# A GRU with the batch turned onto the partitions: split state, 256-column products, biases copied into PSUM, output in rows

## The reference, cut to what matters

```python
# x: [128, 32, 256] f32, cond: [128, 256]; b = 128 sequences of T = 32 steps, D = 256, 16 heads of 16
def block(x, emb):                                   # layer 0, for each sequence by itself
    scale, shift = split(emb @ W_emb + b_emb, 2)
    xn = rms_norm(x, g_norm) * (1.0 + scale) + shift
    q, k, v = heads(xn @ W_qkv)                      # q and k are rms-normed by head
    o = softmax(q @ k.T * 16 ** -0.5) @ v
    return o + o @ W_out
def gru(h, xs):                                      # layer 1, h starts as cond
    for x in xs:                                     # 32 steps
        gi, gh = x @ W_ih + b_ih, h @ W_hh + b_hh    # 256 -> 768 each: r, z, n
        r, z = sigmoid(gi.r + gh.r), sigmoid(gi.z + gh.z)
        n = tanh(gi.n + r * gh.n)
        h = (1 - z) * n + z * h
        yield h
x = x + block(x, cond);  return x + gru(cond, x)
```

## Time and profile before

| what | us |
|---|---|
| median of 3 runs (357.6 to 361.39) | 360.73 |
| the profiled execution's own time | 360.27 |
| span of the profiled execution | 358.5 |
| TensorE busy in the span (94%) | 337.3 |
| DVE, ACT, POOL busy | 251.7, 228.9, 205.2 |
| attention stage, until the last result transpose | 193 |
| first sigmoid of the recurrence | 196.9 |

### The profile page before, as it was taken

The page is one execution under the profiler, slowest core; times in us unless marked ns, Lnnn a source line. Parts: engine busy times, 40 slices in busy tenths (PEclk is TensorE's granted clock), DMA queues, the critical chain, the costliest instruction groups (busy, mean ns, idle before and its releaser), DMA issues.

```text
span 358.5 us, 12899 instructions
## 1 busy us (share of the span) xinstructions
PE 337.3 (94%) x4314; PEld 306.1 (85%) x4314; DVE 251.7 (70%) x637; ACT 228.9 (64%) x668; POOL 205.2 (57%) x381
## 2 busy tenths in 40 slices
PE   7797899999999999999689999999999999999990
PEld 6566788888888888888568999999999999999990
DVE  2658899899999999999775555555555555555554
ACT  3676778888888888876544555555655555655442
POOL 5477777787778777887412454434454444454331
PEclk9999999999999999999999999999999999999997
DMA  5963333232322233255310011211111111111112
GB/s 191 301 202 94 88 86 86 71 89 84 85 83 78 68 86 86 82 153 170 85 33 2 6 30 27 31 27 26 26 27 27 29 26 27 26 26 27 29 30 32
DMA packets 54768, 24.91 MB, mean 69 GB/s; under 512 B 40770, under 2 KB 49620, under 8 KB 54740
## 3 DMA queue, kind: packets, MB, share of 16 engines
q1 hardware_dynamic: 54036, 23.73, 26.7%
q10 hardware_dynamic: 704, 0.82, 0.6%
HBM read 7.48 MB, written 4.19 MB: 33 GB/s over the span
## 4 chain that ended last, share of the span: by engine, by line
PE 80%; SPq 7%; DMA 4%; DVE 2%; POOL 2%; issue 2%; ACT 1%; POOLq 0%; ACTq 0%
PE bank L1047 37%; PE bank L1099 24%; PE bank L1187 4%; PE bank L1206 4%; PE bank L1175 4%; SPq L394 4%; SPq L386 4%; DMA operands<-operands 2%; PE bank L1158 2%; PE bank L1167 2%; DMA w_emb_sb<-in_L_cond_W_emb_dram 1%; PE bank L1066 1%; PE bank L1112 1%; PE bank L1053 1%; POOL operands L457 1%
## 5 line engine op out<-in xcount | busy, mean ns | idle before, releaser
L1099 PE MATMUL bank<-h,w_hh_sb 128*128 128x128 f32 x768 | 95.6, 279 | 0.2
L1099 PEld LDWEIGHTS bank<-h,w_hh_sb 128*128 128x128 f32 x768 | 90.8, 191 | 2.5 <-DVE h L1034 0.8
L1019 DVE SCALAR_TENSOR_TENSOR operands<-bank,vec_cols,operands 128x128 f32<-128x128 f32 x64 | 22.2, 347 | 46.9 <-ACT operands L766 46.9
L1047 PE MATMUL bank<-pair_hi,wih_hi 128*128 128x256 f32 x180 | 52.6, 292 | 0.0
L766 ACT ACTIVATE operands<-bank,bsum 128x128 f32<-128x128 f32 x64 | 23.0, 359 | 46.1 <-PE bank L1099 45.1
L554 POOL TENSOR_TENSOR operands<-operands,h 128x128 f32<-128x128 f32 x64 | 29.6, 463 | 38.3 <-ACT operands L767 38.3
L1047 PE MATMUL bank<-pair_lo,wih_hi 128*128 128x256 f32 x180 | 50.2, 279 | 0.0
L1047 PE MATMUL bank<-pair_hi,wih_lo 128*128 128x256 f32 x180 | 50.1, 278 | 0.0
L563 POOL TENSOR_TENSOR operands<-h,x2T 128x256 f32<-128x256 f32 x31 | 22.5, 727 | 46.7 <-issue 34.1
L1047 PE MATMUL bank<-wqkv_hi,xn_hi 128*128 128x256 f32 (+1 forms) x126 | 47.3, 376 | 0.4 <-POOL xn_lo L486 0.3
L1047 PE MATMUL bank<-wqkv_lo,xn_hi 128*128 128x256 f32 (+1 forms) x126 | 42.4, 336 | 0.0
(11 more groups left out here) (125 smaller groups left out, 855.0 us busy)
## 6 DMA issues: line engine op xcount, KB each, us to landing
v_diag<-v_rows SPq DMA_DIRECT2D x128, 34.0 KB, 1.9
operands<-operands SPq DMA_DIRECT2D x64, 64.0 KB, 2.0
operands<-operands SPq DMA_DIRECT2D x32, 128.0 KB, 2.1
out_dram<-operands SPq DMA_DIRECT2D x254, 16.0 KB, 1.4
x_in<-in_x_dram SPq DMA_DIRECT2D x7, 512.0 KB, 8.9
stage_w<-in_L_cond_W_ih_dram SPq DMA_DIRECT2D x1, 768.0 KB, 5.6
w_hh_sb<-in_L_cond_W_hh_dram SPq DMA_DIRECT2D x1, 768.0 KB, 5.6
w_emb_sb<-in_L_cond_W_emb_dram ACTq DMA_DIRECT2D x1, 512.0 KB, 5.0
```

Of the source, the lines that this page charges most:

```text
L1019: dve.scalar_tensor_tensor(out=rh[:, c, :], in0=xnh[:, HN_COL:HN_COL + B], scalar=bhh[:, 2 * KC + c:2 * KC + c + 1], in1=r_g[:, c, :], op0 ...
L1047: last = pe.matmul(dst, a, w, start=start and i == 0, stop=i == len(terms) - 1, skip_group_check=True)
L1099: last = pe.matmul(dst, gate(w_hh_sb, name, c)[k], moving, start=k == 0 and (name == "n" or opens and name == "z"), stop=k == KC - 1, skip ...
```

## The change

h lies with the batch on partitions, four steps of it in turn. In each step TensorE transposes its two halves (`turned`), ACT writes the high part of each transposed half, DVE the low part, and these are the stationary operands; the weights of w_hh, split into parts in the place of w_qkv, move with 256 columns (r and z of a chunk side by side, or n). So 18 state products in fp32r replace 12 in fp32. The input products have the same turned form, one time step at a time; 13 of the 18 stand before the first transpose, 5 between the two. They belong to the step's own time, not to the next pair. The biases no longer enter as bias columns: products of a row of ones with the bias rows make them in PSUM once for each of two sets of banks, a copy is kept, and in each step ACT copies those of r and z into the banks of the next step, and DVE those of n. z serves for both uses, (z-1)*n being taken from z*h. In the attention stage ACT stores the result x2 to the output in DRAM, two groups at a time; in the recurrence SP loads the rows of a time step from there, POOL adds h, and SP stores them: one load and one store a step. SP places keys before values. POOL copies the high part of a pair in place of ACT. The products without a reader in the recurrence and ahead of it are gone.

Added and changed lines, without their first 12 columns; removed ones are in the functions above.

```diff
...
+wo_parts = sb("wo_parts", [P, 2, KC, D], F32R)
+wo_hi, wo_lo = wo_parts[:, 0, :, :], wo_parts[:, 1, :, :]
+pair_hi = wo_parts
...
+condT = sb("condT", [P, KC, B])
+h = sb("h", [P, 4, D])
+hT_hi = sb("hT_hi", [P, KC, B], F32R)
+hT_lo = sb("hT_lo", [P, KC, B], F32R)
+x2_rows = w_emb_sb[:, :, :].rearrange("p c (s d) -> p (c s) d", s=2)
+cond_sb = h[:, 3, :]
...
+bias_rz = qkn[:, 0, :].rearrange("p (c f) -> p c f", c=KC)
+bias_n = qkn[:, 1, :]
...
+rz_banks = [p.rearrange("p (c f) -> p c f", c=KC)[:, :, 0:2 * P] for p in (p_qk2[:, :], p_s[:, :])]
+n_banks = [p_qkT, p_o]
+hT_banks = [p_xTw[:, 0:P], p_vx2[:, 0:P]]
...
 def body(base, u):
+    g = group(base, u, SP_KEYS)
+    if g is not None:
+        place_keys(g, (u - SP_KEYS) % 2)
     v = group(base, u, SP_V)
     if v is not None:
         place_values(v, (u - SP_V) % 2, (u - SP_V) % 4)
...
     if turn_is(base, u, SP_V):
         load_x(4 * FIRST_SPREAD, NG, x_loaded[FIRST_SPREAD])
     if turn_is(base, u, NG):
         input_gate_weights()
     if turn_is(base, u, NG + 1):
         sp.dma_start(w_hh_sb[:, :, :], w_hh.rearrange("(c p) n -> p c n", p=P)).then_inc(hh_loaded, 16)
+    if turn_is(base, u, NG + 2):
+        for i, vector in enumerate((b_ih, b_hh)):
+            sp.dma_start(bias_row[:, i, :], vector.unsqueeze(0)).then_inc(bias_loaded, 16)
...
+for stored in x2_stored:
+    sp.wait_ge(stored, 16 * (NG // 4))
+def load_rows(t, s):
+    sp.dma_start(x2_rows[:, s, :], out[:, t, :]).then_inc(x2_loaded[s], 16)
+def store_rows(t, s):
+    sp.wait_ge(y_ready, t + 1)
+    sp.dma_start(out[:, t, :], x2_rows[:, s, :]).then_inc(out_done[s], 16)
+def rows(q, s):
+    store_rows(q * 4 + s, s)
+    if later(q, 1) or s >= 2:
+        sp.wait_ge(out_done[(s + 2) % 4], 16 * q + (16 if s >= 2 else 0))
+        load_rows(q * 4 + s + 2, (s + 2) % 4)
...
+    if turn_is(base, u, NG - 3 + POOL_OT):
+        state_weights(0, 0)
+    if turn_is(base, u, NG - 2 + POOL_OT):
+        state_weights(0, 1)
+    if turn_is(base, u, NG - 1 + POOL_OT):
+        state_weights(1, 0)
+        state_weights(1, 1)
+def state_weights(k, half):
+    cols = slice(half * 3 * P, half * 3 * P + 3 * P)
+    pool.wait_ge(whh_hi_ready, 1)
+    pool.tensor_tensor(wqkv_lo[:, k, cols], w_hh_sb[:, k, cols], wqkv_hi[:, k, cols].bitcast(F32),
+                       ALU.subtract).then_inc(whh_lo_ready, 1)
...
+def high_pair(u, slot):
+    pool.tensor_copy(pair_hi[:, slot, :, :], x2T_pair(u)).then_inc(pair_hi_ready, 1)
+def low_pair(u, slot):
     pool.wait_ge(pair_hi_ready, u + 1)
+    pool.sem_inc(pair_high_seen, 1)
...
+        pool.tensor_tensor(zh[:, c, :], z_g[:, c, :], h[:, (s + 3) % 4, c * P:c * P + P],
                            ALU.mult).then_inc(zh_ready[c], 1)
+    pair = (s + 3) // 2
+    if s == 0 or has_pair(base, pair):
+        if s % 2 == 0:
+            low_pair(pair_index(base, pair), pair % 2)
+        else:
+            high_pair(pair_index(base, pair), pair % 2)
     if isinstance(t, int) and t == T - 1:
         return
     pool.wait_ge(h_ready[0], t + 1)
     pool.wait_ge(h_ready[1], t + 1)
...
+    pool.wait_ge(x2_loaded[s], 4 * base + 16)
+    pool.tensor_tensor(x2_rows[:, s, :], h[:, s, :], x2_rows[:, s, :], ALU.add).then_inc(y_ready, 1)
...
+def state_weights():
+    act.wait_ge(hh_loaded, 16)
+    act.wait_ge(qk_ps, NG)
+    act.wait_ge(v_ps, NG)
+    act.copy(wqkv_hi[:, :, :], w_hh_sb[:, :, :]).then_inc(whh_hi_ready, 1)
+def first_state():
+    for c in range(KC):
+        act.copy(hT_hi[:, c, :], condT[:, c, :]).then_inc(hi_ready[c], 1)
+def kept_bias():
+    act.wait_ge(bias_ps, 1)
+    act.copy(bias_rz[:, :, :], rz_banks[0]).then_inc(rz_set, 1)
...
+def store_results(o, slot):
+    act.wait_ge(x2_ready, o + 1)
+    groups = out_groups[:, bass.ds(o - 1, 2), :] if not isinstance(o, int) else out_groups[:, o - 1:o + 1, :]
+    act.dma_start(groups, x2[:, slot - 1:slot + 1, :]).then_inc(x2_stored[slot // 2], 16)
...
+    e = s % 2
+    if later(t, 1):
+        for c in range(KC):
+            act.wait_ge(hT_ps[c], t)
+            act.copy(hT_hi[:, c, :], hT_banks[c]).then_inc(hi_ready[c], 1)
+        if not (isinstance(t, int) and t == T - 1):
+            act.copy(rz_banks[1 - e], bias_rz[:, :, :]).then_inc(rz_set, 1)
+    def reset_gate(c):
+        act.wait_ge(rz_ps[c], t + 1)
+        act.activation(r_g[:, c, :], rz_banks[e][:, c, 0:P], ACT.Sigmoid).then_inc(r_ready[c], 1)
+    def update_gate(c):
+        act.activation(z_g[:, c, :], rz_banks[e][:, c, P:2 * P], ACT.Sigmoid).then_inc(z_ready[c], 1)
+    def new_gate(c):
         act.wait_ge(npre_ready[c], t + 1)
...
+        act.activation(n_g[:, c, :], npre[:, c, :], ACT.Tanh).then_inc(n_ready[c], 1)
+    reset_gate(0)
+    update_gate(0)
+    reset_gate(1)
+    new_gate(0)
+    update_gate(1)
+    new_gate(1)
...
+def first_state():
+    dve.wait_ge(bias_ps, 1)
+    dve.tensor_copy(bias_n[:, :], n_banks[0][:, :]).then_inc(n_set, 1)
+    for c in range(KC):
+        dve.wait_ge(hi_ready[c], 1)
+        dve.tensor_tensor(hT_lo[:, c, :], condT[:, c, :], hT_hi[:, c, :].bitcast(F32),
+                          ALU.subtract).then_inc(lo_ready[c], 1)
...
+    def reset_state(c):
         dve.wait_ge(r_ready[c], t + 1)
...
+        if c == 0:
+            dve.wait_ge(n_ps, t + 1)
+        dve.tensor_tensor(rh[:, c, :], hn[:, cols(c)], r_g[:, c, :], ALU.mult).then_inc(rh_ready[c], 1)
+    def new_input(c):
         dve.wait_ge(rh_ready[c], t + 1)
...
+        dve.tensor_tensor(npre[:, c, :], xn_gate[:, cols(c)], rh[:, c, :], ALU.add)\
+           .then_inc(npre_ready[c], 1)
+    def kept_part(c):
         dve.wait_ge(n_ready[c], t + 1)
...
+        dve.scalar_tensor_tensor(out=zn[:, c, :], in0=z_g[:, c, :], scalar=1.0, in1=n_g[:, c, :],
+                                 op0=ALU.subtract, op1=ALU.mult).then_inc(zn_ready[c], 1)
+    def new_state(c):
         dve.wait_ge(zn_ready[c], t + 1)
         dve.wait_ge(zh_ready[c], t + 1)
...
+        if c == 0 and later(t, 4):
+            dve.wait_ge(y_ready, t - 3)
+        dve.tensor_tensor(h[:, s, cols(c)], zh[:, c, :], zn[:, c, :], ALU.subtract)\
+           .then_inc(h_ready[c], 1)
+    def low_state(c):
+        dve.wait_ge(hi_ready[c], t + 2)
+        dve.tensor_tensor(hT_lo[:, c, :], hT_banks[c], hT_hi[:, c, :].bitcast(F32),
+                          ALU.subtract).then_inc(lo_ready[c], 1)
+    def last_output(c):
+        dve.wait_ge(h_ready[c], T)
+        if c == 0:
+            dve.wait_ge(x2_loaded[3], 16 * (T // 4))
+        dve.tensor_tensor(x2_rows[:, 3, cols(c)], h[:, 3, cols(c)], x2_rows[:, 3, cols(c)],
+                          ALU.add).then_inc(last_y_ready[c], 1)
+    reset_state(0)
+    new_input(0)
+    reset_state(1)
+    kept_part(0)
+    new_input(1)
+    new_state(0)
+    kept_part(1)
+    if last:
+        last_output(0)
+    new_state(1)
+    if last:
+        last_output(1)
+        return
+    for c in range(KC):
+        low_state(c)
+    if not (isinstance(t, int) and t + 2 >= T):
+        dve.tensor_copy(n_banks[e][:, :], bias_n[:, :]).then_inc(n_set, 1)
...
+def gate_columns(weights, k, block):
+    if block == "n":
+        return weights[:, k, 2 * D:3 * D]
+    return weights[:, k, 0:2 * D].rearrange("p (g c a) -> p c g a", g=2, c=KC)[:, block]
+def add_product(dst, moved, weights, k, block):
+    if block != "n":
+        dst = dst.rearrange("p (g a) -> p g a", g=2)
+    return pe.matmul(dst, moved, gate_columns(weights, k, block), start=False, stop=True,
+                     skip_group_check=True)
+def state_block(e, block):
+    return n_banks[e][:, 0:D] if block == "n" else rz_banks[e][:, block, :]
+def input_block(e, block):
+    return n_banks[e][:, D:2 * D] if block == "n" else rz_banks[e][:, block, :]
+def state_high(e, block, k):
+    add_product(state_block(e, block), hT_hi[:, k, :], wqkv_hi, k, block)
+    return add_product(state_block(e, block), hT_hi[:, k, :], wqkv_lo, k, block)
+def state_low(e, block, k):
+    return add_product(state_block(e, block), hT_lo[:, k, :], wqkv_hi, k, block)
+def input_term(e, pair_slot, block, k, term):
+    part, weights = ((pair_hi, wih_hi), (pair_hi, wih_lo), (pair_lo, wih_hi))[term]
+    return add_product(input_block(e, block), part[:, pair_slot, k, e * B:e * B + B], weights, k, block)
+def set_biases(e):
+    pe.wait_ge(bias_loaded, 32)
+    pe.wait_ge(threes_ready, 2)
+    rows = [bias_row[:, i, 0:2 * D].rearrange("p (g c a) -> p c g a", g=2, c=KC) for i in range(2)]
+    for c in range(KC):
+        for i in range(2):
+            pe.matmul(rz_banks[e][:, c, :].rearrange("p (g a) -> p g a", g=2), ones_row[:, :], rows[i][:, c],
+                      start=i == 0, stop=i == 1, skip_group_check=True)
+def set_new_biases(e):
+    pe.matmul(n_banks[e][:, 0:D], ones_row[:, :], bias_row[:, 1, 2 * D:3 * D], start=True, stop=True,
+              skip_group_check=True)
+    return pe.matmul(n_banks[e][:, D:2 * D], ones_row[:, :], bias_row[:, 0, 2 * D:3 * D], start=False,
```

(64 more changed lines are left out.)

275 lines of the change are left out of this document (69 added, 206 removed).

## The result

| | us | ratio to the kernel before (95%) |
|---|---|---|
| before, 4 runs | 361.06 (357.6 to 361.72) | |
| forecast | 350.5 (346.0 to 359.5) | 0.97 |
| after, 4 runs | 373.21 (368.81 to 376.65) | 1.0317 [1.0271, 1.0364] |

The change makes the kernel 3% slower; the forecast had the wrong sign. The ratio leaves out the longest of the four executions after, 376.65 us, which lies more than 1.5% above the fastest. The profiled execution (372.94, span 371.0) splits into three stretches. "h0" is the moment at which the first step's h is complete (both chunks), the steps run from there to the last step's h, the end is what follows. All times are us.

What follows compares the result with a forecast made beforehand. Two nearly equal loops bound a recurrence step: TensorE's products and the chain through h. Start +1.9, steps -9.3, end -2.5 sum to -9.9: span 348.6, plus 1.8 outside 350.4, stated as 350.5 us, range 346 to 359.5.

Steps and rivals of the forecast that it cites:

- some 3 us of 4.6, none of it late: Recurrence step: POOL's z*h, addition and half pair split take some 3 us of 4.6 and delay nothing.
- the price 0.32 for (z-1)n: Recurrence, loop through h: DVE's scalar_tensor_tensor priced between its nearest row 0.347 and the bound 0.29 us.
- The forecast for the steps: 31 recurrence steps at 4.62 us plus 0.1: 143.3 us instead of 152.6, that is -9.3.
- +1.9 forecast: Start of the recurrence: first step's h complete at 202.9 us against 201.03 before.
- 0.8 for the one lump: Start: charge for the first bias set not spread into waits, together with POOL's low part of w_hh delaying the last projection.
- TensorE's 4.58 a step: Recurrence: 36 products at 0.117 us take 4.21, plus two transposes at 0.18 each, 4.58 us a step.
- gates 0.26 and 0.30: Recurrence on ACT: without a bias column a sigmoid takes 0.26 us and a tanh 0.30, against 0.359 and 0.405.
- the end -2.5: After the last h: addition 0.33, one issue 0.46, landing 1.6, 2.4 us in all instead of 4.9.
- Rival A: Recurrence: gates keep their old cost, loop through h stays as long, step 4.90 us; 359 us, chance 0.12.
- Rival B: Recurrence: copies of biases into PSUM take three times the read, 1.8 us, step 5.3; 371.5 us, chance 0.11.
- Rival C: Attention loop: ACT's stores or later values stall TensorE 0.3 to 0.6 us a turn; 355.5 to 359.5 us, chance 0.09.
- The 0.12 for slower: Chance that the change is slower: slow bias copies into PSUM, with some weaker form of them.

Runs made afterwards that it cites:

- experiment 1: Changed kernel with POOL's pair split placed behind its y addition instead of ahead of it; 354.99 us, ratio 0.9863.
- experiment 7: Changed kernel with POOL's pair split behind the y addition and the bias products made from 128 rows instead of one; 350.6 us, ratio 0.97.
- experiment 2: Changed kernel with ACT's tanh written into PSUM instead of SBUF; 363.32 us, ratio 1.0036.
- experiment 3: Kernel before: pair split moved ahead of the y addition, 360.48 us; instead an unread POOL subtraction added behind the second z*h in odd steps, 367.24 us.
- experiment 4: Changed kernel with the same twelve fp32 bias products made from 128 rows instead of one; 368.54 us, ratio 1.0234.
- Experiment 8: Changed kernel with late pair split and 128-row bias products, w_ih and w_hh loaded in turns 8 and 10: 351.94 us; second bias set also copied: 351.95 us.
- experiment 6: Changed kernel with the second set of bias products replaced by four fp32r products and copies by ACT and DVE; 370.0 us, ratio 1.0306.

## Why the prediction was wrong

**The step that failed** is the sentence "POOL has z*h twice, an addition like the old one and half a pair split: some 3 us of 4.6, none of it late", together with the price 0.32 for (z-1)n. It asked whether POOL's work is in time. It did not ask what POOL's work does to DVE while it runs. By the placing in the code the half split starts right behind the second z*h, when tanh 1 ends: exactly over (z-1)n and h of chunk 1, the end of the loop through h. The kernel before has that split too (all of it in every second step), but behind the y addition, where DVE has at most one operand in SBUF or stands still; so its (1-z)n shows 0.292 as a mean over 64 and nothing warns. The forecast for the steps was 143.3 us; without the collision they take 142.0 and 142.18 (experiments 1 and 7), with it 157.95, and experiments 2 and 3 show that it is this collision: moving one operand to PSUM moves the hold to the next operation, and an extra POOL operation at that place makes the steps of the kernel before 6.55 us longer.

**The second failure** is the start: +1.9 forecast, +9.6 measured. The sets' duration was right (2.8). What the sum had no term for is the clock, 0.52 on average over 184 to 196 us. The 9.6 fall apart like this. With both edits h0 is at +2.7. The clock costs 6.2 (experiments 4 and 7, 4.4 of it between the two sets and 1.8 behind the second). The collision costs 0.95 in step 0: from h of chunk 0 to h of chunk 1 go 1.73 in experiment 4 and 0.78 in experiment 7. The rest, -0.2, is mostly that the first set happens to start a little sooner (181.97 against 182.12 in experiment 7). What lets the clock fall in the changed kernel and not in the kernel before is shown as far as the rows of the products go; that it also fell behind waits, without such products, leaves open what exactly is needed.

The 0.8 between 2.7 and 1.9 lies ahead of the second set, which starts at 194.09 in experiment 7 and was put at 192.96. TensorE's waits for key blocks are as long as in the kernel before (3.7 us in all between 150 and 200 us in both), but its waits for DVE's attention result ahead of the transposes have grown from 1.0 to 2.6. This is where the first state products of before had stood in four parts, and where the prediction charged 0.8 for the one lump; that reading is of the trace alone, and no run tests it. Experiment 8 only excludes the weight loads.

**What held**, each by its own step: TensorE's 4.58 a step (measured 4.58; 4.62 allowed 0.04 for two equal loops, which was not needed: TensorE alone is the bound, and in experiment 1 h of chunk 1 ends at 242.49, 0.31 ahead of its transpose at 242.80, so the loop through h was priced about 0.3 too long); gates 0.26 and 0.30 (0.277, 0.307); bias copies hidden; the attention loop at no loss; the end -2.5 (-2.44). Rival A, the loop through h keeping its length for the price of the gates, did not come; the loop did become the longer one, by another cause. Rival B, slow copies into PSUM, gave a time near the measured one (371.5) and is refuted: 0.60 and 0.68. A close number is no evidence for its mechanism. Rival C did not come. And the 350.6 us of experiment 7 is in part luck: its steps are 1.1 us shorter than forecast and its start 0.8 longer, which nearly cancel.

**The chances.** Nothing in the forecast had a place for two engines sharing a path. The 0.12 for slower hung on one mechanism only. The lower bound of 346 also lies 1 us below its own terms (31 x 0.05 for a step of 4.57, and 2 for the start, give 347), which changes nothing here.

## What to carry to other kernels

When work is moved on POOL, look up which DVE operations it will lie over; those with two operands in SBUF ended just behind POOL's in every run here, so the longest POOL operation belongs where DVE has at most one operand in SBUF. When a mean duration in a group is above that of its form, compare the ends with those of the other engine before looking for a cause in the operation. For products that only fill a bank (biases times ones), try a form with all 128 rows and compare the granted clock behind them: here the products took no longer and the start was 6.2 us shorter between the first set and h0.

## What the runs showed that was not expected

- Held DVE operations end 0.14 to 0.15 us behind POOL's, for lengths of 0.40, 0.56, 0.73, 0.95 and 1.23 instead of 0.29. The profile shows the hold as duration of the DVE operation, not as a wait. POOL's cast with one operand in SBUF holds DVE as its subtraction with two does.
- One row instead of 128 in fp32 products of the same count, columns and duration: mean granted clock 0.965 to 0.988 against 0.993 to 1.0 in the changed kernel, 0.971 to 0.982 against 0.995 to 0.997 with the late pair split. The fall is not the same in each profiled execution: 0.50 from 185 to 198 and from 202 to 205 us in the changed kernel, without a break from 185 to 205 in experiment 2. In the kernel before, without such products, the executions have 0.982 to 0.996, so smaller falls occur in it too.
- A set of products that stands alone on TensorE can be the cover of a wait: its 2.3 us came back as 1.68 (experiment 6).
